# Six copies per attention unit, the gate's square roots as powers on GpSimd, and a re-planned order of tasks

## The reference

```python
def tok(src):                                   # six gated convolutions
    x = (emb_table[src] @ W_e2h + b_e2h).T
    for i in range(6):
        a, g = split(conv1d_same(x, conv_w[i], conv_b[i]))      # 3 taps, 128 -> 256
        x = (a * sigmoid(g) + x) * 0.7071
    return x.T @ W_h2e + b_h2e
def attn(x):                                    # 8 heads of 16, two score maps each
    attn1, attn2 = softmax(q1 @ k1.T / 4), softmax(q2 @ k2.T / 4)
    # of windows of 4 rows: mean, std (ddof=1), max, min of each map's rows
    gate_in = concat([window_stats(attn1), window_stats(attn2)])
    alpha = sigmoid(relu(relu(gate_in @ gw1 + gb1) @ gw2 + gb2) @ gw3 + gb3)
    return heads((alpha * attn1 + (1 - alpha) * attn2) @ v) @ Wo
def ffn(x):                                     # 8 experts by position, exact gelu
    xa = (norm(x) * ln_g + ln_b) @ attn_w.T + attn_b + x
    y = gelu(xa @ fc1_w[e].T + fc1_b[e]) @ fc2_w[e].T + fc2_b[e]
    return gelu(y @ next_w.T + next_b)
h = tok(x);  h = h + attn(norm(h));  h = h + ffn(norm(h))
```

## Time and profile before

| | |
|---|---|
| median of three runs | 5781.32 us (5776.51 to 5792.61) |
| the profiled execution: own time, span | 5777.35 us, 5775.5 us |
| busy: PE, DVE, ACT, POOL | 5177.0, 5109.5, 5196.2, 2454.1 us |
| granted clock of TensorE, mean | 0.963 |
| DMA | 140.83 MB, mean 24 GB/s |

### The profile page before, as it was taken

How to read it: one execution, slowest core, us unless ns; L and a number is a source line. 1 busy time by engine, 2 the same in 40 slices (tenths; PEclk the granted TensorE clock), 3 DMA queues, 4 the chain that set the end, 5 groups by cost and what they waited for, 6 DMA issues and landing times.

```text
span 5775.5 us, 120393 instructions
## 1 busy us (share of the span) xinstructions
PE 5177.0 (90%) x33798; PEld 2429.7 (42%) x33798; DVE 5109.5 (88%) x7715; ACT 5196.2 (90%) x7903; POOL 2454.1 (42%) x4439
## 2 busy tenths in 40 slices
PE   6998989899898998989889898998989899898995
PEld 4443434344343443434334343443434344343442
DVE  1989899898999989899898999989899898989983
ACT  2999999999999999999989999999999999999994
POOL 6525344352533525344352534525344352534523
PEclk8999999999999999999999999999999999999997
DMA  1001010010101001010010101001010010101000
GB/s 35 23 20 31 20 32 20 22 28 19 31 20 32 19 19 32 18 32 21 22 29 21 31 19 31 20 19 32 18 32 21 22 28 21 32 19 30 21 22 14
DMA packets 164931, 140.83 MB, mean 24 GB/s; under 512 B 89196, under 2 KB 108268, under 8 KB 164140
## 3 DMA queue, kind: packets, MB, share of 16 engines
q1 hardware_dynamic: 159100, 124.09, 9.3%
q0 software_dynamic: 4352, 8.92, 0.7%
q10 hardware_dynamic: 816, 0.02, 0.0%
HBM read 21.26 MB, written 8.91 MB: 5 GB/s over the span
## 4 chain that ended last, share of the span: by engine, by line
PE 41%; ACT 21%; issue 17%; POOL 10%; DVE 8%; SPq 2%; DMA 1%; ACTq 1%; POOLq 1%; DVEq 0%
PE ps_w L395 18%; PE ps_t L395 9%; ACT junk L587 9%; PE ps_o L395 7%; ACT exps L594 6%; PE ps_s L395 6%; DVE neg_s L726 3%; ACT hpre L598 2%; SPq L336 2%; DVE rowmin L734 1%; DVE bn L746 1%; POOL part L881 1%; POOL ctmp L1013 1%; POOL part L1015 1%; ACT stage L598 1%
## 5 line engine op out<-in xcount | busy, mean ns | idle before, releaser
L726 DVE TENSOR_SCALAR_CACHE_REDUCE neg_s<-ps_s 128x1024 f32<-128x1024 f32 x2048 | 2492.4, 1217 | 389.8 <-PE ps_s L395 338.3
L734 DVE TENSOR_REDUCE rowmin<-neg_s 128x1 f32<-128x1024 f32 x2049 | 2479.4, 1210 | 0.0
L587 ACT ACTIVATE junk<-neg_s,negmax 128x1024 bf16<-128x1024 f32 x2048 | 2357.9, 1151 | 112.8 <-DVE neg_s L726 106.4
L594 ACT ACTIVATE exps<-ps_t 128x1024 f32<-128x1024 f32 x2060 | 2116.0, 1027 | 179.7 <-PE ps_t L395 174.6
L395 PE MATMUL ps_t<-qst,kst 99*128 99x512 bf16 x4120 | 1274.4, 392 | 235.8 <-ACT exps L594 232.7
L395 PE MATMUL ps_o<-exps,v_cur 128*32 128x256 f32 x16512 | 1351.2, 400 | 143.8 <-DVE o_raw L742 120.8
L395 PE MATMUL ps_s<-kst,qst 96*128 96x512 bf16 x4096 | 1255.3, 388 | 67.3 <-DMA kst<-part 59.0
L395 PE MATMUL ps_w<-xc,cw 128*128 128x256 f32 x4704 | 1158.0, 382 | 3.7 <-DVE z L799 2.7
L395 PEld LDWEIGHTS ps_w<-xc,cw 128*128 128x128 f32 x4704 | 888.8, 190 | 221.2 <-DVE z L799 10.6
L395 PEld LDWEIGHTS ps_o<-exps,v_cur 128*32 128x32 f32 x16512 | 329.0, 109 | 1055.5 <-issue 643.0
L881 POOL TENSOR_SCALAR ctmp<-ug 128x256 f32<-128x256 f32 x408 | 165.8, 406 | 1331.4 <-ACT ug L663 1312.1
(11 more groups left out here) (181 smaller groups left out, 3932.8 us busy)
## 6 DMA issues: line engine op xcount, KB each, us to landing
qst<-part SPq DMA_DIRECT2D x1542, 32.0 KB, 2.0
kst<-part SPq DMA_DIRECT2D x1542, 32.0 KB, 2.0
qst<-mrow SPq DMA_DIRECT2D x1028, 1.5 KB
out_dram<-z SPq DMA_DIRECT2D x17, 512.0 KB, 3.2
fc1s<-in_fc_w SPq DMA_DIRECT2D x17, 256.0 KB
fc2s<-in_fc_w SPq DMA_DIRECT2D x17, 256.0 KB
cw<-in_conv_w SPq DMA_DIRECT2D x1, 2304.0 KB
odif<-in_table,idx POOLq DMA_INDIRECT x136
```

Of the source, the lines that this page charges most:

```text
L587: nc.scalar.activation(junk[:, n % 2, :], neg_s[:, n % SLOTS_S, :], ACT.Exp, scale=-1.0, bias=negmax[:, r, t:t + 1], accum_out=sumsq[:, r, ...
L594: nc.scalar.activation(exps[:, n % RING, :], ps_t[:, :, :].rearrange("p c q -> p (c q)"), ACT.Exp, scale=0.5).then_inc(s_exp, 1)
L726: nc.vector.tensor_scalar(neg_s[:, n % SLOTS_S, :], ps_s[:, n % 2, :], -1.0, None, ALU.mult, ALU.min, accum_out=negmax[:, r, t:t + 1]).the ...
L734: nc.vector.tensor_reduce(rowmin[:, r, t:t + 1], neg_s[:, m % SLOTS_S, :], axis=AX, op=ALU.max, negate=True).then_inc(s_min, 1)
```

## The change

The three parts of a query or key land by six copies, three with the queries repeated by a zero stride and three with keys in a run of parts; the queries' copies wait for the queries' chains alone. The two Sqrt activations are replaced by eight GpSimd powers of 128x16 elements, one a step task `std`, spaced by two steps (in the tail one behind the other). ln3 has no moments: as the mean of a normed row is zero, its variance is var x rstd^2, made of ln2's by GpSimd in small operations, followed by one wide multiplication. The planner has new costs and no longer keeps conv halves of PRE out of steps with `std`.

By the planner's loop these steps hold the tasks before -> after: std 21 -> 21, 23, 25, ... 35; win 23 -> 38; hid1 25 -> 40; alpha 32 -> 48; attT 36, 37 -> 52, 53; ln2 41 -> 57; ln3 48 -> 64; fc1 65 to 79 -> 81 to 95; gelu1 80 -> 96; ln1 and gelu2 108 -> 106; qk of the next sequence 116 to 122 -> 114 to 120. Conv halves in steps 26 to 37: before at 26, 28, 30, 31, 33, 34, 35, after at 26 to 34, 36, 37.

```diff
-Q_PART = (0, 0, 0, 1, 1, 2)
-K_PART = (0, 1, 2, 0, 1, 0)
+RUNS = ((0, 3), (3, 2), (5, 1))
+LOADS = 2 * len(RUNS)
...
+STD = [("std", k) for k in range(U // 2)]
...
-POOL_COST = {..., "snap": 80, ..., "ln3": 66, ...}
-STEP_WEIGHT = 27
+POOL_COST = {..., "snap": 115, ..., "ln3": 50, "std": 30, ...}
+STEP_WEIGHT = 25
...
-                if task[0] in ("conva", "convg") and behind > STEP_WEIGHT:
+                if task[0] in ("conva", "convg") and behind > 2 * STEP_WEIGHT:
                     break
-                if stage is pre and any(t[0] in ("gelu1", "gelu2", "std") for t in at[n]):
+                if stage is pre and any(t[0] in ("gelu1", "gelu2") for t in at[n]):
...
-                for g in range(NPART):
-                    for dst, w, c in ((qst, 0, Q_PART[g]), (kst, 1, K_PART[g])):
-                        sp.dma_start(dst[HD * g:HD * g + HD, r, :], part[HD * h:HD * h + HD, a, w, c, :])\
+                for c, (g, count) in enumerate(RUNS):
+                    src = part[HD * h:HD * h + HD, a, 0, c, :]
+                    sp.dma_start(qst[HD * g:HD * (g + count), r, :],
+                                 src.unsqueeze(1).to_broadcast([HD, count, L])).then_inc(s_ring[r], 16)
...
+                for g, count in RUNS:
+                    sp.dma_start(kst[HD * g:HD * (g + count), r, :], part[HD * h:HD * h + HD, a, 1, 0:count, :])\
+                      .then_inc(s_ring[r], 16)
...
-                            wait_side(sp, "body", i, "pool", QK[(j + 1) % U // H][-1])
-                        load_unit((j + 1) % U)
+                        for part_of, load in ((1, load_q), (3, load_k)):
+                                wait_side(sp, "body", i, "pool", QK[(j + 1) % U // H][part_of])
+                            load((j + 1) % U)
...
                 if kind == "win":
-                    w("act", ("std",))
+                    w("pool", STD[-1])
...
-                elif kind == "ln3":
-                    w("pool", ("ln2",))
-                    last = moments(i, x2, 1)
...
+                elif kind == "std":
+                    a, h = tk[1] // (H // 2), tk[1] % (H // 2) * 2
+                    last = tt(gin[:, :, h:h + 2, 4 * a + 1].rearrange("p t h -> p h t"),
+                              gtmp[:, 3, T * (H * a + h):T * (H * a + h + 2)].rearrange("p (h t) -> p h t", h=2),
+                              half_pow[:, :, :], ALU.pow)
...
-                    last = normalise(i, att, x2, 1)
+                    chain(i, tt(rstd[:, 1, :], mv[:, 0, :, 1], rstd[:, 0, :], ALU.mult))
+                    chain(i, tt(rstd[:, 1, :], rstd[:, 1, :], rstd[:, 0, :], ALU.mult))
+                    chain(i, ts(rstd[:, 1, :], rstd[:, 1, :], 1.0, EPS, ALU.mult, ALU.add))
+                    chain(i, tt(rstd[:, 1, :], rstd[:, 1, :], rs_pow[:, :], ALU.pow))
+                    last = tt(att[:, :, :], x2[:, :, :], rstd[:, 1, :].unsqueeze(2).to_broadcast([P, T, P]), ALU.mult)
```

More of the change, by code:

```diff
@@ L60 @@
 PRE = [("gather",)] + two("embT") + two("e2h") + CONV + two("h2e") + [("ln1",)] + two("xnT") + QK[0] + two("v")
-POST = ([("snap",), ("std",), ("win",), ("hid1",), ("hid2",), ("logit",), ("alpha",)] + two("attT") + two("wo")
+STD = [("std", k) for k in range(U // 2)]
+POST = ([("snap",)] + STD + [("win",), ("hid1",), ("hid2",), ("logit",), ("alpha",)] + two("attT") + two("wo")
         + [("ln2",), ("ln3",)] + two("nT") + [("attw", c) for c in range(NC)]
@@ L66 @@
     "msplit": ("pool",), "mrow": ("dve",), "unit": ("dve", "pool"), "vcopy": ("pool",), "hcopy": ("pool",), "snap": ("dve", "pool", "act"),
-    "std": ("act",),
+    "std": ("pool",),
     "win": ("pe", "dve"), "hid1": ("pe", "dve"), "hid2": ("pe", "dve"), "logit": ("pe", "act", "pool"),
     "alpha": ("pe", "dve", "pool"), "attT": ("pe", "act"), "wo": ("pe", "dve"), "ln2": ("dve", "pool"),
-    "ln3": ("dve", "pool"), "nT": ("pe", "act"), "attw": ("pe", "act"), "fc1": ("pe", "act"), "gelu1": ("act",),
+    "ln3": ("pool",), "nT": ("pe", "act"), "attw": ("pe", "act"), "fc1": ("pe", "act"), "gelu1": ("act",),
     "fc2": ("pe", "act"), "fc2p": ("pe",), "next": ("pe", "dve"), "gelu2": ("act", "pool"), "gather": (), "embT": ("pe", "act"),
@@ L80 @@
         "qk": 9, "v": 9}
-POOL_COST = {"msplit": 8, "unit": 5, "qk": 35, "convg": 23, "gather": 85, "snap": 80, "alpha": 46, "hcopy": 20,
-             "ln1": 66, "ln2": 66, "ln3": 66, "gelu2": 24, "vcopy": 15}
-STEP_WEIGHT = 27
-GAP = {("std",): 5, ("win",): 2, ("hid1",): 2, ("hid2",): 2, ("logit",): 2, ("alpha",): 2, ("attT", 0): 4,
+POOL_COST = {"msplit": 8, "unit": 5, "qk": 35, "convg": 23, "gather": 85, "snap": 115, "alpha": 46, "hcopy": 20,
+             "ln1": 66, "ln2": 66, "ln3": 50, "std": 30, "gelu2": 24, "vcopy": 15}
+STEP_WEIGHT = 25
+GAP = {("std", 0): 5, ("win",): 3, ("hid1",): 2, ("hid2",): 2, ("logit",): 2, ("alpha",): 2, ("attT", 0): 4,
        ("wo", 0): 2, ("ln3",): 5, ("nT", 0): 6, ("attw", 0): 2, ("gelu1", 0): 1, ("gelu1", 1): 0, ("gelu1", 2): 0, ("gelu1", 3): 0, ("fc2", 0): 0, ("next", 0): 2,
@@ L89 @@
        **{task: 2 for task in QK[0]}}
-SPREAD = {"attw": 2, "fc1": 2}
+SPREAD = {"attw": 2, "fc1": 2, "std": 2}
 SLOTS = {"ln1": (2, 3, 4), "ln2": (0, 1, 2, 3, 4), "ln3": (0, 1, 2, 3), "alpha": (0, 1, 2, 3, 4),
@@ L202, in tower_kernel @@
         rs_pow = sb("rs_pow", [P, T])
+        half_pow = sb("half_pow", [P, 2, T])
         part = sb("part", [P, 2, 2, 3, L], BF16)
@@ L329, in load_ids, with load_q, load_k @@
                 sp.dma_start(idx[:, :], ids[b]).then_inc(s_idx, 16)
-            def load_unit(u):
+            def load_q(u):
                 a, h, r = u // H, u % H, u % RING
-                for g in range(NPART):
-                    for dst, w, c in ((qst, 0, Q_PART[g]), (kst, 1, K_PART[g])):
-                        sp.dma_start(dst[HD * g:HD * g + HD, r, :], part[HD * h:HD * h + HD, a, w, c, :])\
-                          .then_inc(s_ring[r], 16)
+                for c, (g, count) in enumerate(RUNS):
+                    src = part[HD * h:HD * h + HD, a, 0, c, :]
+                    sp.dma_start(qst[HD * g:HD * (g + count), r, :],
+                                 src.unsqueeze(1).to_broadcast([HD, count, L])).then_inc(s_ring[r], 16)
+            def load_k(u):
+                a, h, r = u // H, u % H, u % RING
+                for g, count in RUNS:
+                    sp.dma_start(kst[HD * g:HD * (g + count), r, :], part[HD * h:HD * h + HD, a, 1, 0:count, :])\
+                      .then_inc(s_ring[r], 16)
             def store_mrow(phase, i, j):
@@ L362, in _ @@
                 sp.dma_start(dst, src).then_inc(s_load, 16)
-            wait_side(sp, "pre", 0, "pool", QK[0][-1])
-            load_unit(0)
+            wait_side(sp, "pre", 0, "pool", QK[0][1])
+            load_q(0)
+            wait_side(sp, "pre", 0, "pool", QK[0][3])
+            load_k(0)
             with sp.Fori(0, NB // E) as group:
@@ L379, in _ @@
                         store_mrow("body", i, j)
-                        if j + 1 in (U // 2, U):
-                            wait_side(sp, "body", i, "pool", QK[(j + 1) % U // H][-1])
-                            settle()
-                        load_unit((j + 1) % U)
+                        for part_of, load in ((1, load_q), (3, load_k)):
+                            if j + 1 in (U // 2, U):
+                                wait_side(sp, "body", i, "pool", QK[(j + 1) % U // H][part_of])
+                                settle()
+                            load((j + 1) % U)
                         if ("gelu2",) in sum((STEP[n] for n in range(j * T, j * T + T)), []):
@@ L400, in scores @@
                 if t == 0:
-                    pe.wait_ge(s_ring[u % RING], i * (4 * 12 * 16) + 12 * 16 * (u // RING + 1))
+                    pe.wait_ge(s_ring[u % RING], i * (4 * LOADS * 16) + LOADS * 16 * (u // RING + 1))
                 pe.wait_ge(s_max, i * STEPS + n + 1)
@@ L614, in task @@
                                                 ACT.Exp, scale=0.5)
[L615 to L621, removed]
                 elif kind == "logit":
@@ L831, in _ @@
             nc.vector.memset(rs_pow[:, :], -0.5)
+            nc.vector.memset(half_pow[:, :, :], 0.5)
             nc.vector.memset(xc[:, :, 0:1], 0.0)
@@ L844, in _ @@
                 task("pre", 0, tk)
-            pos.update(loop=True, base=pos["n"], n=0, per=3)
+            pos.update(loop=True, base=pos["n"], n=0, per=2)
             with dve.Fori(0, NB // E) as group:
@@ L965, in task @@
                     chain(i, tt(gtmp[:, 1, :], gtmp[:, 2, :], gtmp[:, 1, :], ALU.subtract))
-                    ts(gtmp[:, 3, :], gtmp[:, 1, :], 1.0 / (L - 1), 0.0, ALU.mult, ALU.max)
+                    ts(gtmp[:, 3, :], gtmp[:, 1, :], 1.0 / (L - 1), 1e-30, ALU.mult, ALU.max)
                     heads = lambda t: t[:, :, :].rearrange("p t (h d) -> p t h d", h=H)
@@ L987, in task @@
                 elif kind == "ln3":
-                    w("dve", tk)
                     w("pe", ("attT", 1))
```

(5 more changed lines are left out.)

## The result

The changed kernel takes 5806.39 us (median of 5 runs, 5803.9 to 5822.33) against 5781.32: a ratio of 1.005, 95% interval 1.0031 to 1.0068. It is slower by half a per cent, by more than the 0.3% that can be told from no change. The profiled execution is the slowest of the five, 5822.33 us, 16 above the median, so the traces differ by 45 us where the medians differ by 25.

What follows compares the result with a forecast made beforehand. Floors per step were VectorE 2.27 us and TensorE 2.84 with a conv half; GpSimd's queue would decide steps 17 to 38. 16 x (3.9 - 0.7 - 1.3 + 0.5) - 14 - 5.7 + 21 = +40 on 5777.35: 5817, written 5815; range 5725 to 5860.

Steps and rivals of the forecast that it cites:

- the cheap root: Rival: a power costs per instruction, so GpSimd's queue stops deciding steps 17 to 38; 5700 us, chance 0.18 shared with unseen gains.
- Its largest term: Steps 17 to 38: GpSimd's queue through the eighth root delays win; stretch 62.8 us against 58.91, +3.9 a sequence.
- the rival of half cost: Rival for steps 17 to 38: a root of 2.75 us or overlapping ends takes 2.8 a sequence off; 5769 us, chance 0.2.
- 1 to 3 us a sequence: TensorE's granted clock may fall after idle spells, adding 16 to 45 us in total; counted only in the range.
- I cost this at nothing: Removing ScalarE's square roots and two table loads, 3.05 us a sequence, was to gain 0, being covered by neg_s slots.
- The rival that they were on the path: Rival: ScalarE's square roots delay exponentials in steps 17 to 38, so removal saves 3.05 us a sequence; 5768 us, chance 0.12.
- 0.7 and 1.3 less 0.5: Steps 39 to 127, per sequence: third norm -0.7, VectorE's earlier msplit 14 -1.3, ScalarE's copy behind ln2 +0.5.
- Copies: Six copies end TensorE's wait: 0.95 us in steps 127 and 0, fifteen times (-14), and 5.7 off the first load.
- Tail: After the last step: eight roots in a row +25 us, shorter third norm -3.9, together +21 (+10 with cheap roots).

## Why the prediction was right, and where it was not

**The forecast** was 5815, slower, because GpSimd's queue from the snapshot to the eighth root sets the end of steps 17 to 38. Mechanism and sign are shown: the queue has no pause, `mparts`, `va` and `win` are the waits that were named, and shorter roots take the loss away at 1.66 us already, below the 2.4 that the cheap root was given as its bound. Step by step the loss stands where it was said to: VectorE's `mrow` waits 2.32 us at step 24 (2.6 forecast) and 2.77 at step 32 (5 forecast), ScalarE's copy 2.2 at step 35.

**Its largest term was right by luck**, by errors that cancel. +3.9 a sequence was forecast and 4.15 measured, but the queue ends at 59.6, not at 61.9: the root takes 2.93 us, not 3.11, and 3.16 from its start to the next instruction (1963.44 to 1966.60 above), not 3.35, which is 1.5 in eight; units and msplits are a little shorter too. Against that, step 39 begins 1.75 us behind the root and not 0.9, as `win`'s matmuls take 1.05 and the scores must follow before the scan. By the queue alone the stretch lasts 61.4, +2.5, between the forecast and the rival of half cost. The other 1.7 is TensorE at its lower clock behind the idle spell, which the prediction named (1 to 3 us a sequence) but put in the range and not in the sum. That this came out slower, and not as no change, hung on it: 16 x 1.7 is 27 us, and the profiled execution without them would stand 18 above that of before, where 17 is the least that can be told from no change. That TensorE had to stand still followed from its own list of waits: a copy that waits for a chain, exponentials queued behind it. The sum should have carried a cost there.

**"I cost this at nothing"**, said of the square roots, failed. VectorE's scan had no idle time behind them, as stated, but TensorE's `ps_t` did, 0.96 us, and this row was not read. The rival that they were on the path had the mechanism right (exponentials that come late), at a third of its 3.05 us in the old plan; in the new plan the square roots would cost 2.0. The Trainium skill's figure (ScalarE: Activation LUTs, Table sets: the hidden batching unit), about 5.3 us for the two loads, would by estimate be some 85 us in sixteen sequences; the loads take 1.28 each, and 18.8 us were gained.

**Third norm and plan.** Steps 39 to 127 were to gain 1.5 us (0.7 and 1.3 less 0.5) and gained 1.74, 1.47 without step 127, again with the parts shifted: the norm alone gives 1.6 in steps 39 to 127, and the changed kernel there is only 0.4 below copies and norm in the old plan. VectorE's wait for msplit 14 at step 112 is gone (3.56 to 2.40), but step 120 takes 3.86 for 3.28. So the norm may account for nearly all of the gain, and what its long step gives back was then taken too large; in the new plan no run takes the norm alone away, so this is not shown.

**Copies**: 0.95 and 5.7 forecast; 1.1 (0.84 and 0.27) and 4.9 measured. But the 0.95 was to lie in steps 127 and 0, and these gave 0.5; the rest came from steps 1 to 16, for which nothing was counted. In the kernel before TensorE's clock is at its lower level at the start of all fifteen later sequences, behind the wait for the copies, for 61 us of their steps 0 to 16 together; in the changed kernel for 4. So part of what the copies gave is the clock, which the prediction did not count here either; how much of it was not measured by itself. **Tail**: +21 forecast, +22.3 measured; eight roots take 23.90 us there, for 25.6:

```profile
5725.14 23.90 POOL L980 TENSOR_TENSOR gin<-gtmp,half_pow 128x16 f32<-128x16 f32 x8
```

**What stays open.** Why three of sixteen sequences keep the full clock behind the same idle of 2.48 us; and why the profiled execution is 16 us above its median. Sequences that differ by up to 3 us in this way could do it, but the mean granted clock speaks against it: 0.963 in the profiled execution, and 0.963 also in those of 5805 and 5806 us. Only one execution has a trace.

## What to carry to other kernels

Work moved to an idle engine is judged in the stretch where it lands: add up that engine's queue there, in order, to the first result that somebody waits for, and compare the end with what the other engines need; until then it costs nothing (roots of 1.66 us), from then on what lies above. When TensorE has to stand still for a few microseconds, add the clock behind it to the sum, and where a change takes such a wait away, expect the clock back too. Before a removed operation is costed at nothing, look at the next wait of every engine that its own engine feeds, not of one.

## What the runs showed of the hardware

- GpSimd's power costs by columns: 1656 ns for 128x8 and 2929 for 128x16, by these two sizes some 0.16 us a column and 0.4 beside it.
- The same 124 MB in fewer and larger copies (the queries' with the source repeated by a zero stride) took 15.6% of the DMA engines' time where it took 9.3%, with 134428 packets for 159100; a copy of 96 KB lands after 2.7 to 2.9 us, one of 32 KB took 2.0. Behind the first load no engine waits for these copies here.
- Behind the same idle spell of 2.5 us TensorE's granted clock fell in thirteen sequences of the changed kernel and not in three; behind 2.15 us, with four conv buffers, also in thirteen; behind the 2.2 to 5.0 us before each sequence of the kernel before in all fifteen.
